# Two pairs' masks loaded once and spread by VectorE, all weight masking on GpSimd, and the first group's products behind all eight units

## What is computed

```python
# x (32, 256, 256), cond (32, 8), weight (8, 256, 256), mask (256, 256), bias (256)
masked_w = weight * mask[None, :, :]
w_bot = jnp.einsum('bg,got->bot', cond, masked_w)
return x + jnp.einsum('bnt,bot->bno', x, w_bot) + bias
```

## Time and profile before

| | |
|---|---|
| three runs | 66.37, 66.73, 66.96 us |
| median | 66.73 us |
| span of the profiled execution | 65.5 us |
| the median less that span (start and end around it) | 1.2 us |
| PE busy, DVE busy, ACT busy, POOL busy | 58.8, 48.1, 47.9, 7.0 us |
| stage 1 and 2: first group's products end, group 1 begins | 22.84 us into the span |
| groups 1 to 7 on TensorE | 22.84 to 62.3 us |

### The profile page before, as it was taken

The page is one execution under the profiler, slowest core; times in us unless marked ns, Lnnn a source line. Parts: engine busy times, 40 slices in busy tenths (PEclk is TensorE's granted clock), DMA queues, the critical chain, the costliest instruction groups (busy, mean ns, idle before and its releaser), DMA issues.

```text
span 65.5 us, 1501 instructions
## 1 busy us (share of the span) xinstructions
PE 58.8 (90%) x645; PEld 54.3 (83%) x645; DVE 48.1 (73%) x36; ACT 47.9 (73%) x40; POOL 7.0 (11%) x17
## 2 busy tenths in 40 slices
PE   2997188999999999999999999999999999999910
PEld 1266087977888899999999999999999999999900
DVE  2109809999957989999999999989999992250200
ACT  2506609799889999999999799999869986005520
POOL 5500299900000000000000000000000000000000
PEclk9999999999999999999999999999999999999999
DMA  0999999999998157954999999999999229918393
GB/s 0 260 373 306 352 412 422 407 434 428 420 410 340 60 85 255 408 215 198 245 285 225 400 451 420 403 441 423 398 413 425 93 100 408 398 63 325 158 372 116
DMA packets 5334, 20.21 MB, mean 309 GB/s; under 512 B 592, under 2 KB 1104, under 8 KB 4432
## 3 DMA queue, kind: packets, MB, share of 16 engines
q1 hardware_dynamic: 5040, 19.89, 79.6%
q10 hardware_dynamic: 288, 0.23, 1.1%
HBM read 11.73 MB, written 8.39 MB: 307 GB/s over the span
## 4 chain that ended last, share of the span: by engine, by line
PE 79%; DMA 9%; ACT 4%; SPq 2%; issue 1%
PE slots L433 20%; PE slots L431 20%; PE slots L432 20%; PE slots L451 11%; DMA weights<-in_first 9%; PE slots L332 6%; ACT w_raw L534 3%; PE slots L326 2%; ACT weights L563 1%; SPq L230 1%; SPq L222 1%; SPq L229 1%
## 5 line engine op out<-in xcount | busy, mean ns | idle before, releaser
L431 PE MATMUL slots<-x_hi,w_hi 128*128 128x256 f32 x112 | 31.4, 280 | 0.0
L432 PE MATMUL slots<-x_lo,w_hi 128*128 128x256 f32 x112 | 31.2, 279 | 0.0
L433 PE MATMUL slots<-x_hi,w_lo 128*128 128x256 f32 x112 | 31.2, 279 | 0.0
L431 PEld LDWEIGHTS slots<-x_hi,w_hi 128*128 128x128 f32 x112 | 21.1, 188 | 0.0
L432 PEld LDWEIGHTS slots<-x_lo,w_hi 128*128 128x128 f32 x112 | 21.1, 188 | 0.0
L433 PEld LDWEIGHTS slots<-x_hi,w_lo 128*128 128x128 f32 x112 | 21.1, 188 | 0.0
L589 DVE TENSOR_TENSOR x_lo<-x_ring,x_hi 128x2048 fp32r<-128x2048 f32 (+1 forms) x8 | 16.1, 2022 | 0.5 <-ACT x_hi L491 0.5
L491 ACT CAST x_hi<-x_ring 128x2048 fp32r<-128x2048 f32 (+1 forms) x8 | 13.5, 1694 | 1.3 <-DMA x_ring<-in_x 1.3
L511 ACT ACTIVATE weights<-slots,smalls 128x1024 f32<-128x1024 f32 x10 | 10.8, 1112 | 4.7 <-PE slots L433 4.7
L598 DVE TENSOR_TENSOR w_lo<-w_raw,w_hi 128x2048 fp32r<-128x2048 f32 x6 | 13.7, 2288 | 0.2 <-ACT w_hi L499 0.2
L499 ACT CAST w_hi<-w_raw 128x2048 fp32r<-128x2048 f32 x6 | 11.5, 1909 | 0.0
(11 more groups left out here) (25 smaller groups left out, 19.3 us busy)
## 6 DMA issues: line engine op xcount, KB each, us to landing
out<-weights SPq DMA_DIRECT2D x15, 512.0 KB, 4.7
x_ring<-in_x SPq DMA_DIRECT2D x7, 1024.0 KB, 9.6
x_ring<-in_first SPq DMA_DIRECT2D x6, 512.0 KB, 7.2
weights<-in_first SPq DMA_DIRECT2D x4, 256.0 KB, 6.6
out<-weights SPq DMA_DIRECT2D x1, 256.0 KB, 2.4
out<-weights SPq DMA_DIRECT2D x1, 128.0 KB, 2.3
out<-weights ACTq DMA_DIRECT2D x1, 128.0 KB, 2.1
smalls<-in_small ACTq DMA_DIRECT2D x1, 97.0 KB, 3.1
```

Of the source, the lines that this page charges most:

```text
L431: nc.tensor.matmul(dst, wh, xh, start=(k == 0), stop=False)
L432: nc.tensor.matmul(dst, wh, xl, start=False, stop=False)
L433: last = nc.tensor.matmul(dst, wl, xh, start=False, stop=(k == KC - 1))
```

## The change

- **Loads.** The masks of pairs 0 and 1 no longer come with every weight row. Eight successive partitions hold the eight weights of the same output row and so need the same mask row; an array `in_mask` of 128 KB has each of those rows once, and is loaded first, into `compact`. Weights of pair 0 come as two loads of 256 KB; for pairs 1 to 3 the diagonal and the other weights of a pair come in one load of 512 KB, followed for pairs 2 and 3 by a mask load of 256 KB. x of group 0 is one load of 1 MB. x of group 2 is loaded without a wait; only x of group 3 waits for the masking.
- **Spreading.** DVE copies `compact` to the mask rows by four `stream_shuffle` instructions of 128 x 256, where DVE masked pair 0 before.
- **Masking.** All four pairs are masked by POOL, in place (L297 of the changed kernel). DVE masks no weights ahead of the mixing.
- **Order.** All eight units run in a row; the 16 products of group 0 follow whole. The first output half of group 1's weights is split in one piece instead of two (`pieces`), after unit 7 on ACT and DVE. Group 0's first result is stored to SBUF by one ACT instruction instead of two. The PSUM slots of the products are numbered anew.

```diff
-EARLY = 6
...
-ORDER = (("other", 0), ("masked", 0), ("masked", 1), ("other", 1), ("off", 0), ("masked", 2), ("other", 2), ("x", 0),
-         ("masked", 3), ("other", 3), ("x", 1))
-COLUMNS = {"masked": SLOT, "other": BANK, "off": (UNITS - SIDES) * SPAN, "x": WIDE // 2}
+ORDER = (("other", 0), ("masked", 0), ("pair", 1), ("off", 0), ("pair", 2), ("mask", 2), ("pair", 3), ("mask", 3), ("x", 0))
+COLUMNS = {"masked": BANK, "other": BANK, "pair": SLOT, "mask": BANK, "off": (UNITS - SIDES) * SPAN, "x": WIDE}
...
+SPREAD = 2
+COMPACT = BANK // 2
+CHUNKS = SPREAD * BANK // COMPACT
...
+        compact = sb("compact", [P, COMPACT])
...
-        def staged(j):
-            return x_ring[:, XS - 2 + j // 2, (j % 2) * SLOT:(j % 2 + 1) * SLOT]
+        mask_rows = x_ring[:, XS - 1, :]
+        def mask_half(c):
+            return mask_rows[:, c * COMPACT:(c + 1) * COMPACT]
...
-        pieces = ((0, NB // 2, 0), (NB // 2, NB, 0), (0, NB, 1))
+        pieces = ((0, NB, 0), (0, NB, 1))
...
-            return slots[:, (1, 0, 3, 2)[(2 * g + h) % SLOTS], :]
+            return slots[:, (3, 0, 1, 2)[(2 * g + h) % SLOTS], :]
         def unit_slot(u, side):
             if u < SIDES:
                 return slots[:, 2 * u + side, :]
-            if u < EARLY:
-                return slots[:, ((0, 3), (1, 2))[u % 2][side], :]
-            return slots[:, ((0, 1), (3, 2))[u % 2][side], :]
-        early = slots[:, 3, 0:BANK]
...
-                sp.dma_start(staged(j), in_order("masked", j)).then_inc(masked_loaded[j], 16)
-                sp.dma_start(blocks[:, 2 * j + 1, :], in_order("other", j)).then_inc(others_loaded[j], 16)
-            def load_half(i):
-                return sp.dma_start(x_ring[:, 0, i * SLOT:(i + 1) * SLOT], in_order("x", i))
-            sp.dma_start(blocks[:, 1, :], in_order("other", 0)).then_inc(others_loaded[0], 16)
-            sp.dma_start(staged(0), in_order("masked", 0)).then_inc(masked_loaded[0], 16)
+                sp.dma_start(weights[:, j, :], in_order("pair", j)).then_inc(pair_loaded[j - 1], 16)
+                if j >= SPREAD:
+                    sp.dma_start(mask_rows[:, j * BANK:(j + 1) * BANK], in_order("mask", j)).then_inc(mask_loaded[j - SPREAD], 16)
+            sp.dma_start(compact[:], mask).then_inc(compact_loaded, 16)
+            sp.dma_start(blocks[:, 1, :], in_order("other", 0)).then_inc(first_others_loaded, 16)
+            sp.dma_start(blocks[:, 0, :], in_order("masked", 0)).then_inc(first_masked_loaded, 16)
             load_pair(1)
             sp.dma_start(masks_off[:].rearrange("p u m r -> p (u m r)"), in_order("off", 0)).then_inc(masks_off_loaded, 16)
             load_pair(2)
-            load_half(0).then_inc(half_x_loaded, 16)
             load_pair(3)
-            load_half(1).then_inc(x_loaded[0], 16)
+            sp.dma_start(x_ring[:, 0, :], in_order("x", 0)).then_inc(x_loaded[0], 16)
             load_group(1)
-            sp.wait_ge(masked_by_dve, 2)
-            sp.wait_ge(masked_by_pool, 2)
-            load_group(XS - 2)
-            sp.wait_ge(masked_by_pool, 2 * (PAIRS - 2))
-            sp.wait_ge(masked_by_dve, 4)
+            load_group(2)
+            sp.wait_ge(masked_by_pool, 2 * PAIRS)
             load_group(XS - 1)
...
-            behind_pair = (None, (0,), (1, 2, 3))
-            for j in range(1, PAIRS - 1):
-                pool.wait_ge(masked_loaded[j], 16)
+            def mask_pair(j):
+                pool.wait_ge(first_masked_loaded if j == 0 else pair_loaded[j - 1], 16)
+                if j >= SPREAD:
+                    pool.wait_ge(mask_loaded[j - SPREAD], 16)
                 for i in range(2):
-                    nc.gpsimd.tensor_tensor(blocks[:, 2 * j, half_of(i)], staged(j)[:, 0:BANK][:, half_of(i)],
-                                            staged(j)[:, BANK:SLOT][:, half_of(i)], ALU.mult).then_inc(masked_by_pool, 1)
-                if j == 1:
-                    pool.wait_ge(smalls_loaded, 16)
-                    pool.wait_ge(raw_by_act, 1)
-                for i in behind_pair[j]:
-                    some = raw_columns(1, False)[:, i * MB:(i + 1) * MB, :]
-                    nc.gpsimd.tensor_tensor(some, some, smalls[:, AT_MASKS + SPAN:AT_MASKS + 2 * SPAN].unsqueeze(1).broadcast_to(
-                        [P, MB, SPAN]), ALU.mult).then_inc(raw_masked, 1)
+                    if j < SPREAD:
+                        pool.wait_ge(mask_spread, 2 * j + i + 1)
+                    nc.gpsimd.tensor_tensor(blocks[:, 2 * j, half_of(i)], blocks[:, 2 * j, half_of(i)],
+                                            mask_half(2 * j + i), ALU.mult).then_inc(masked_by_pool, 1)
+            def mask_raw(i):
+                some = raw_columns(1, False)[:, i * MB:(i + 1) * MB, :]
+                nc.gpsimd.tensor_tensor(some, some, smalls[:, AT_MASKS + SPAN:AT_MASKS + 2 * SPAN].unsqueeze(1).broadcast_to(
+                    [P, MB, SPAN]), ALU.mult).then_inc(raw_masked, 1)
+            mask_pair(0)
+            mask_pair(1)
+            pool.wait_ge(smalls_loaded, 16)
+            pool.wait_ge(raw_by_act, 1)
+            mask_raw(0)
+            mask_pair(2)
+            mask_pair(3)
+            for i in range(1, B // MB):
+                mask_raw(i)
...
-                    if u == EARLY and q % 2 == 0:
-                        pe.wait_ge(masked_by_dve, 3 + q // 2)
-                    elif u % 2 == 0 and q % 2 == 0:
-                        pe.wait_ge(masked_by_pool, u - 1 + q // 2)
+                    if u % 2 == 0 and q % 2 == 0:
+                        pe.wait_ge(masked_by_pool, u + 1 + q // 2)
...
-            for u in range(SIDES, EARLY):
+            for u in range(SIDES, UNITS):
                 weigh_unit(u)
-            pe.wait_ge(raw_by_act, EARLY - 1)
+            pe.wait_ge(raw_by_act, UNITS - 1)
             pe.wait_ge(raw_by_dve, UNITS // HO)
             pe.wait_ge(raw_masked, 1)
-            pe.wait_ge(half_x_loaded, 16)
-            multiply_first(early, 0, 0, NB // 2).then_inc(early_ready, 1)
-            for u in range(EARLY, UNITS):
-                weigh_unit(u)
-            pe.wait_ge(raw_by_act, UNITS - 1)
             pe.wait_ge(x_loaded[0], 16)
-            multiply_first(product(0, 0)[:, BANK:SLOT], 0, NB // 2, NB).then_inc(products_ready, 1)
+            multiply_first(0)
             pe.wait_ge(raw_by_act, UNITS)
             pe.wait_ge(raw_by_dve, UNITS)
-            multiply_first(product(0, 1), 1, 0, NB).then_inc(products_ready, 1)
+            multiply_first(1)
...
-                if u == EARLY:
-                    act.wait_ge(raw_by_act, UNITS // HO)
-                    act.wait_ge(raw_by_dve, UNITS // HO)
-                    act.wait_ge(raw_masked, 1)
-                    high_piece(0)
-                    high_piece(1)
-                    act.wait_ge(smalls_loaded, 16)
-                    act.wait_ge(early_ready, 1)
-                    nc.scalar.activation(result(0, 0)[:, 0:BANK], early, ACT.Identity, bias=bias(0)).then_inc(early_by_act, 1)
                 act.wait_ge(diagonal_ready, u + 1)
                 nc.scalar.copy(raw_slot(u, True), made(u, True)).then_inc(raw_by_act, 1)
+            act.wait_ge(raw_by_act, UNITS // HO)
+            act.wait_ge(raw_by_dve, UNITS // HO)
+            act.wait_ge(raw_masked, 1)
+            high_piece(0)
             act.wait_ge(raw_by_act, UNITS)
             act.wait_ge(raw_by_dve, UNITS)
-            high_piece(2)
+            high_piece(1)
...
-            act.wait_ge(products_ready, 1)
-            nc.scalar.activation(result(0, 0)[:, BANK:SLOT], product(0, 0)[:, BANK:SLOT], ACT.Identity,
-                                 bias=bias(0)).then_inc(out0_by_act, 1)
+            act.wait_ge(smalls_loaded, 16)
+            finish(0, 0, out0_by_act)
...
-            def mask_pair(j):
-                dve.wait_ge(masked_loaded[j], 16)
-                for i in range(2):
-                    nc.vector.tensor_tensor(blocks[:, 2 * j, half_of(i)], staged(j)[:, 0:BANK][:, half_of(i)],
-                                            staged(j)[:, BANK:SLOT][:, half_of(i)], ALU.mult).then_inc(masked_by_dve, 1)
-            mask_pair(0)
+            dve.wait_ge(compact_loaded, 16)
+            for c in range(CHUNKS):
+                nc.vector.stream_shuffle(mask_half(c), compact[:], [G * (i // G) + c for i in range(ROWS)]).then_inc(mask_spread, 1)
...
-                    mask_pair(PAIRS - 1)
-                    low_piece(0)
-                    low_piece(1)
...
-            low_piece(2)
+            low_piece(0)
+            low_piece(1)
```

More of the change, by code:

```diff
@@ L50, with conditional_residual @@
 SMALL = AT_MASKS + SIDES * SPAN
-def conditional_residual(nc, x, small, first, out):
+SPREAD = 2
+COMPACT = BANK // 2
+CHUNKS = SPREAD * BANK // COMPACT
+def conditional_residual(nc, x, small, mask, first, out):
     assert QU * P == BANK and SLOT == 2 * BANK and O == N == T and QU * B * RT == BANK
```

(26 more changed lines are left out.)

37 lines of the change are left out of this document (10 added, 27 removed).

## The result

The changed kernel took 69.95 us (median of four, 69.05 to 80.44), the kernel before 66.76 us on the same chip: ratio 1.0415, 95% interval 1.0332 to 1.0499. Forecast were 66.1 us and a range of 65.3 to 67.1. The change makes the kernel slower by 4%, and none of the rivals named its cause.

The account below looks back on a forecast made before the run. Group 1's start on TensorE, set by pair 1's landing, POOL, unit 2, ACT and unit 4, was taken as the bound. Gains of 0.37 and 0.23 made 0.6 us: span 64.9, plus 1.2, gives 66.1 us; range 65.3 to 67.1.

Parts of the forecast that it names:

- What bounds the kernel: TensorE runs without a gap from group 1's start at 22.84 us, so the question is when group 1 can start.
- The base: The trace's own span of 65.5 us, plus 1.2 us that the median of the runs has above the span.
- pair 1 earlier, 0.37: Pair 1 lands at 7.35 instead of 7.65, so mixing of unit 2 ends at 9.4, 0.37 us earlier.
- target of 10.63 for unit 4: TensorE starts unit 4 at 10.63 us, where the profile before had 11.00.
- Masked 0: 128 KB less ... 0.3 us earlier: 4.7: Pair 0's load, 128 KB smaller at 357 to 415 GB/s, lands at 4.7 us instead of 4.99.
- a delay of single engines is added: Pair 1's landing waits for the slowest of 16 DMA engines; such a delay doesn't shrink with the load, hence 7.35 us.
- Shuffles: DVE's four 128 x 256 shuffles take 0.42 us each from about 3.4 us and end at 5.1.
- POOL slower than DVE, "covered": POOL masks at 0.71 us a step against DVE's 0.38; TensorE's later end of units 0 and 1, 6.75, is covered.
- The order, 0.23 gained: All 32 early matmuls of group 0 run in one block of 6.79 us, saving 0.23 us by not stopping between.
- x in time: Group 0's x, in one load, lands at 15.2 us, before TensorE needs it at 15.47.
- splits of group 1 with slack: ACT and DVE finish group 1's splits by 21.2 us, 1.05 before group 1 starts; moving them behind unit 7 costs nothing.

Follow-up runs that it names:

- g0: The kernel before, unchanged, profiled a second time and compared with itself: 66.26 us, ratio 0.994.
- k3: The kernel before with six warm-up matmuls instead of five: 66.57 us, ratio 1.003 against the kernel before.
- e0: The changed kernel, unaltered, in a second comparison with the kernel before, for an undisturbed profile: 69.75 us, ratio 1.042.
- f2: The changed kernel with the compact load issued on ACT's queue behind the small load, not on SP's: 67.54 us, ratio 1.015 against the kernel before.
- h2: The kernel before, its loads and masking kept, with the changed kernel's order of units, x load, products and weight piece: 67.78 us, ratio 1.013.
- f3: The changed kernel with eight matmuls of zeros, adding nothing, where TensorE waited for POOL: 68.17 us, ratio 1.021 against the kernel before.
- m1: The changed kernel with compact on ACT's queue, the old order of units, x halves and pieces, and DVE masking pair 3: 67.32 us, ratio 1.012.

## Why the prediction was wrong, point by point

- **What bounds the kernel: right.** Group 1's start decided, and the 42.6 us behind it stayed as they were.
- **The base: wrong.** The sum was made on an execution 1 us longer than the usual one, with "1.2 us that the median has above the span". What lies around the span is 1.8 (1.74 to 1.84 in the 27 executions of the comparisons of g0), and in the executions near the median (g0, k3) the span is 64.5 and 64.7. There unit 4 starts at 9.80 and 9.94, in g0 with POOL released at 6.50; it is not 11.00 and 7.71. The term "pair 1 earlier, 0.37" thus shortened a delay that only some executions have: the kernel before already beat the target of 10.63 for unit 4.
- **"Masked 0: 128 KB less ... 0.3 us earlier: 4.7": the step that failed.** It landed at 7.20, and at 5.58 to 7.87 in all runs with a load ahead on SP's queue. The step counted bytes by a rate. But one more load stood ahead, whose issue moved that of masked 0 from 1.17 to 1.63; the rate itself was lower than the 357 to 415 GB/s that the step took (277 and 299 in the windows above); and a landing waits for the last of 16 engines: in e0 fifteen had their share at 5.16, the last at 7.20. Between 4.4 and 7.1 us single packets took 0.5 to 1.2 us. The prediction had this thought for pair 1 ("a delay of single engines is added") and did not apply it to masked 0. With 4.7 replaced by 7.20, its own terms give pair 0's second half at 8.6 and the rest of the wait.
- **The clock: missing.** No rival had TensorE standing idle and its clock falling behind that. Cost 1.56. Nor did the sum have a term for the mixing ahead of the clock's rise: the execution it was built on had the full clock from 3.95, the usual ones (g0, k3) from 6.2.
- **Shuffles: right.** 0.435 to 0.441 each, a step of 0.34, from 3.13; forecast 0.42 from 3.4. The Trainium skill's "VectorE: DVE Perf Modes", section on the perf-mode tier table, gave by proportion an estimated 0.3, less than the 0.44 measured and near the step of 0.34.
- **POOL slower than DVE, "covered": right for the rate** (0.71 a step as forecast), wrong for the cover. In f2 POOL masks pairs 0 and 1 back to back from 5.45 to 8.24, though pair 1 had landed by 6.8; in g0, where DVE has pair 0, POOL is done with pair 1 at 7.92.
- **The order, 0.23 gained: wrong in sign where TensorE is early.** The products in one block came as forecast (6.79; 18.07 to 24.89 is 6.82). But the early products were the cover for DVE's mask of pair 3 in before and for a stop inside unit 6. "Where the cover is gone" had not been asked of them. On before's loads the order costs 1.3% (h2, 0.4 to 2.1%). In e0 itself, where unit 4 was late, the stretch was 0.32 shorter than in g0.
- **x in time, splits of group 1 with slack: right.** TensorE never waited for x, nor for a split of group 1. At 18.07, x (landed 15.1) had been there for 3 us.
- **Sum of the loss,** e0 less g0: unit 4 later 3.35, stretch shorter 0.32, around the span 0.2: 3.2 of the 3.2 us between the two executions (69.53 - 66.31). Of the 3.35, 1.56 is the clock; the rest, 1.8, goes to the late landing. f3, late but at full clock, supports that: its unit 4 is 1.72 behind g0's.

No version beat the kernel before. The best that keeps the compact load is m1 at 67.32.

## What to carry to other kernels

Before a load is put at the head of a queue, ask which landing it pushes back and who starves: the first transfer that releases the main engine should stay first, and an addition goes to another queue. Judge a landing by its last engine, not by bytes over rate, and profile the same kernel twice before a term is built on a stall of half a microsecond. Check a clock of 1.00 by the pace of like matmuls: it may only mean that nothing was recorded yet. A block of work that stands between two others may be there as cover; price its removal by what would show beneath it.
